# Three edits to an eight-core transformer-layer kernel: the rope's PSUM copy issued from ScalarE, one more wait ahead of the local attention, and the accumulate of the last feed-forward product written in place

## What is computed

```python
x = x + layernorm(attention(layernorm(x)))
x = x + layernorm(ffn(layernorm(x)))
```

```python
hidden = sigmoid(x @ q(w1).T) * (x @ q(w2).T)      # 5632 features
out = hidden @ q(w3).T
```

## Time and profile before

| | |
|---|---|
| median of 2 timed runs | 5871.52 us (5860.42 to 5882.63) |
| the profiled execution, its own time | 5821.73 us |
| its span, slowest core (7) | 5820.1 us; the eight cores 5774.1 to 5820.1 us |
| around the span | 1.6 us |
| busy on core 7 | PE 2818.6 us, DVE 2440.4 us, ACT 858.0 us, POOL 271.8 us |

### The profile page before, as it was taken

The page is one execution under the profiler, slowest core; times in us unless marked ns, Lnnn a source line. Parts: engine busy times, 40 slices in busy tenths (PEclk is TensorE's granted clock), DMA queues, the critical chain, the costliest instruction groups (busy, mean ns, idle before and its releaser), DMA issues.

```text
span 5820.1 us, 37163 instructions; the slowest of 8 cores (5774.1 to 5820.1 us)
## 1 busy us (share of the span) xinstructions
PE 2818.6 (48%) x11251; PEld 1090.7 (19%) x11251; DVE 2440.4 (42%) x3412; ACT 858.0 (15%) x1049; POOL 271.8 (5%) x518
## 2 busy tenths in 40 slices
PE   1556555556555522222222223657467676745553
PEld 1111111111111111111111111103223232322221
DVE  5322222222222244444444443004554545467887
ACT  1211122221122211111111111431100000000001
POOL 0000000000000001111111110000000000000000
PEclk9776666667766655555555555558688888877777
DMA  5211111111111033333333332013122222222221
GB/s 117 44 23 23 29 23 20 20 20 24 30 25 19 7 86 76 76 76 76 76 76 76 76 77 49 0 32 92 58 94 94 92 97 91 98 94 80 73 73 72
DMA packets 107475, 346.76 MB, mean 60 GB/s; under 512 B 12432, under 2 KB 69904, under 8 KB 78480
## 3 DMA queue, kind: packets, MB, share of 16 engines
q0 software_dynamic: 74016, 107.77, 12.8%
q1 hardware_dynamic: 17712, 123.38, 5.9%
q10 hardware_dynamic: 15552, 113.25, 5.5%
HBM read 443.71 MB, written 8.39 MB: 78 GB/s over the span
## 4 chain that ended last, share of the span: by engine, by line
PE 43%; DVE 27%; DMA 12%; ACT 9%; issue 8%; DVEq 1%; POOL 0%; ACTq 0%; POOLq 0%; SPq 0%
DMA AB<-w_t 10%; ACT MID L467 8%; PE pSA L888 7%; PE pSB L888 5%; DVE STT L281 4%; DVE STT L299 4%; PE pSA L450 3%; PE pAVB L497 3%; PE pAVB L394 3%; PE pT L345 3%; PE pSA L394 3%; PE pSA L969 2%; PE pG L516 2%; PE pSA L665 2%; PE pSB L394 2%
## 5 line engine op out<-in xcount | busy, mean ns | idle before, releaser
L345 PE MATMUL pT<-IDE,MID 128*128 128x128 bf16 x1216 | 153.8, 306 | 1233.2 <-DVE MID L325 1155.1
L281 DVE TENSOR_REDUCE STT<-AB 128x1 f32<-128x704 bf16 x384 | 340.1, 886 | 508.7 <-DMA AB<-w_t 495.2
L888 PE MATMUL pSA<-MID,WQS 128*128 128x512 bf16 x1408 | 400.4, 455 | 283.7 <-DVE WQS L871 283.7
L467 ACT ACTIVATE MID<-pSA,BIA 128x1024 bf16<-128x1024 f32 x212 | 236.3, 1115 | 1533.0 <-PE pSB L450 1533.0
L497 PE MATMUL pAVA<-MID,AB 128*65 128x512 bf16 x424 | 209.8, 595 | 353.7 <-ACT MID L467 208.3
L345 PEld LDWEIGHTS pT<-IDE,MID 128*128 128x128 bf16 x1216 | 117.7, 138 | 1266.2 <-issue 1266.2
L475 DVE TENSOR_TENSOR MID<-MID,AUX 128x1024 bf16<-128x1024 bf16 x128 | 88.6, 692 | 620.7 <-ACT MID L467 620.6
L969 PE MATMUL pSA<-WQS,AB 128*128 128x512 bf16 x576 | 171.5, 429 | 307.8 <-DVE AUX L948 238.7
L888 PE MATMUL pSB<-MID,WQS 128*128 128x512 bf16 x1408 | 311.1, 379 | 0.0
L450 PE MATMUL pSA<-MID 64*128 64x512 bf16 x300 | 151.3, 605 | 304.6 <-DVE STT L288 287.1
L279 POOL DMA_DIRECT2D AB<-w_t x384 | 203.0, 529 | 1838.8 <-DVE STT L288 1787.0
(11 more groups left out here) (137 smaller groups left out, 4086.6 us busy)
## 6 DMA issues: line engine op xcount, KB each, us to landing
AB<-w_t POOLq DMA_DIRECT2D x384, 176.0 KB, 3.4
AUX<-w_t ACTq DMA_DIRECT2D x66, 1024.0 KB, 4.8
XS<-w_t SPq DMA_DIRECT2D x66, 1024.0 KB, 4.8
MID<-x_glob SPq DMA_DIRECT2D x36, 1024.0 KB, 6.3
XS<-x_glob ACTq DMA_DIRECT2D x36, 1024.0 KB, 4.8
WQS<-wq_t POOLq DMA_DIRECT2D x16, 512.0 KB, 6.0
WQS<-wk_t POOLq DMA_DIRECT2D x15, 512.0 KB, 5.0
WQS<-wv_t POOLq DMA_DIRECT2D x15, 512.0 KB, 5.0
```

The costliest lines, as they stand in the source:

```text
L281: em("V", lambda e, par=par: e.tensor_reduce(ACOL, absbuf(par), AX.X, ALU.add, apply_absolute_value=True))
L345: tok = em("T", lambda e, dc=dc, k=k: e.transpose(pT[:, k * 128:(k + 1) * 128], XLT[:, dc * 128:(dc + 1) * 128], IDE[:]), "T" if k == 7 el ...
L467: e.activation(expsl(hb, 0, par), pbuf[:], AF.Exp, bias=b, scale=0.125),
L888: e.matmul(pbank[:, th * 512:(th + 1) * 512], w12q(m, qpar)[:, dc * 128:(dc + 1) * 128], xln2(dc, th * 512, (th + 1) * 512), start=(dc == ...
```

## The change

1. In `rope_chunk` the copy out of PSUM is an ACT activation with the function Copy instead of a DVE copy. It waits on ACT for the product, for the last rotation matmul and for the DVE instruction that last read `RAW0` (a new entry `rope_V` in `state`); PE and DVE wait for ACT's token where they used DVE's own order. The shapes are 128x512 in the local stage and 128x256 in the global one. Everything else of the chunk stays on its engine.
2. Ahead of the loop over pairs PE waits for all that DVE and ACT have been given so far.
3. In the second feed-forward product the add of groups 1 to 8 writes straight into `acct`, which is also its second input; the copy behind it (L985) is gone, and the bank's token is the add's.

```diff
--- before.py
+++ after.py
@@ -329,6 +329,7 @@
             return tn
 
         state = {"evac": 0, "xg_war": 0, "xlt_war": 0, "rot_T": 0,
+                 "rope_V": 0,
                  "xs_v": [0, 0], "xs_a": [0, 0], "cg_war": [0, 0]}
 
         def ln_transpose_tile(src_ap, src_tok, dst3, dst_col, pp):
@@ -398,17 +399,21 @@
             return tok
 
         def rope_chunk(psum_ap, pkey, cos_ap, sin_ap, dst_ap, ptok, W=512):
-            wt("V", "T", ptok)
-            wt("V", "T", state["rot_T"])
-            t_raw = em("V", lambda e, ps=psum_ap, W=W: e.tensor_copy(
-                RAW0[:, 0:W], ps), "V")
-            wt("T", "V", t_raw)
+            wt("A", "T", ptok)
+            wt("A", "T", state["rot_T"])
+            wt("A", "V", state["rope_V"])
+            t_raw = em("A", lambda e, ps=psum_ap, W=W: e.activation(
+                RAW0[:, 0:W], ps, AF.Copy), "A")
+            wt("T", "A", t_raw)
             psum_wait(["pG"])
             t_rot = em("T", lambda e, W=W: e.matmul(
                 pG[:, 0:W], RP[:], RAW0[:, 0:W], start=True, stop=True), "T")
             state["rot_T"] = t_rot
-            em("V", lambda e, cos_ap=cos_ap, W=W: e.tensor_tensor(
-                RTMP[:, 0:W], RAW0[:, 0:W], cos_ap, ALU.mult))
+            wt("V", "A", t_raw)
+            state["rope_V"] = em("V", lambda e, cos_ap=cos_ap, W=W:
+                                 e.tensor_tensor(
+                                     RTMP[:, 0:W], RAW0[:, 0:W], cos_ap,
+                                     ALU.mult), "V")
             wt("V", "T", t_rot)
             em("V", lambda e, sin_ap=sin_ap, W=W: e.tensor_tensor(
                 RAW1[:, 0:W], pG[:, 0:W], sin_ap, ALU.mult))
@@ -546,6 +551,8 @@
             wload(i, order[i][1], order[i][0])
         next_w = 4
         wt("T", "V", tv_ones)
+        wt("T", "V", cnt["V"])
+        wt("T", "A", cnt["A"])
         t_attn_T = 0
         for p in range(NPAIR):
             sq, sk, sv = (3 * p) % 4, (3 * p + 1) % 4, (3 * p + 2) % 4
@@ -978,12 +985,11 @@
                                      acct(tc)[:, hs * 512:(hs + 1) * 512],
                                      pb), "V")
                     else:
-                        em("V", lambda e, tc=tc, hs=hs, pb=pb:
-                           e.tensor_tensor(
-                               TMP6, pb,
-                               acct(tc)[:, hs * 512:(hs + 1) * 512], ALU.add))
-                        tev = em("V", lambda e, tc=tc, hs=hs: e.tensor_copy(
-                            acct(tc)[:, hs * 512:(hs + 1) * 512], TMP6), "V")
+                        tev = em("V", lambda e, tc=tc, hs=hs, pb=pb:
+                                 e.tensor_tensor(
+                                     acct(tc)[:, hs * 512:(hs + 1) * 512], pb,
+                                     acct(tc)[:, hs * 512:(hs + 1) * 512],
+                                     ALU.add), "V")
                     PW[pk] = ("V", tev)
                 if glast:
                     pp = tc % 2
```

## The result

| | before | after |
|---|---|---|
| median | 5851.22 us (5804.93 to 5884.26, 10 runs) | 5845.42 us (5744.41 to 5897.85, 11 runs) |
| ratio, 95% interval | | **0.985 [0.98, 0.99]** |
| profiled execution, its own time | 5821.73 us | 5758.61 us |
| its span; mean of the eight cores | 5820.1; 5795.8 us | 5757.0; 5733.5 us |
| busy on the slowest core | PE 2818.6, DVE 2440.4, ACT 858.0 us | PE 2779.7, DVE 2299.2, ACT 915.5 us |

In some executions the cores of one die show a lower clock whatever the kernel is; the ratio leaves these out, so it is not the quotient of the two medians. The change is faster by 1.5%, within the 2% called "the same". The forecast was 0.992 of before. Times of before reach down to 5804.93 us and times of after to 5744.41 us, 60.5 us apart, and the two profiles are 63.1 us apart; the forecast had 45.3.

The account below looks back on a forecast made before the run. No engine is full on average; work passes hand to hand, with DVE pacing feed-forward groups 1 to 7. Terms 27.9 + 11.4 + 7.3 + 1.5 - 2.8 = 45.3 us less, median 5826 us, range 5785 to 5862 us.

Parts of the forecast that it names:

- The accumulate in place: Second feed-forward product: without the copy PE paces groups 1 to 7, saving 27.9 us; the last group saves 11.4 us.
- The mis-sized term: Groups 1 to 7 of the second feed-forward product become like group 0: 3.99 us less a group, 27.9 us.
- the other reading in the prediction: Same groups, read from first instruction to quantization, 39.76 against 35.42 us: 4.34 a group, 30.4 us as upper reading.
- The rope's copy on ACT, local: Local stage rope chunks, 128x512: ACT copy 597 ns instead of DVE's 692, all on the chain, 77 chunks, 7.3 us less.
- the rival with no gain on ACT: Rope chunks: handover or copy on ACT eats the 0.095 us; gain 36.5 us, median 5835 us; 10 in 100.
- The rope's copy on ACT, global: Global stage rope chunks, 128x256: ACT copy an estimated 378 ns instead of DVE's 425, 32 chunks, 1.5 us less.
- The wait ahead of the pairs: Start of local stage: PE's first product waits for DVE's last sum, starting at 165.2 instead of 162.4; costs 2.8 us once.
- The Square pass and the tables: Global Square pass some 10 us later, covered by ACT's idle time; table-switch rival, 122 us of loads, 2 in 100.
- The full price: Rival, second feed-forward product: DVE alone paces, 256 copies at 0.40 us give 102 us; median 5763 us; 2 in 100.
- The 13/16: Cited clock rule, second feed-forward groups: dense matmuls on three or more cores of a die; tile 1.33 us, median 5884 us.
- the only one that spoke of the clock: Rival, groups 1 to 7: PE loses clock without its rests; at 1.2 GHz median 6066 us, slower; 3 in 100.
- The base: Whole kernel: profiled 5821.7 us less 45.3 gives 5776.4, ratio 0.992, scaled onto the 5871.5 us median: 5826 us.

Follow-up runs that it names:

- e2_local: Kernel before with the rope copy on ACT for the 128x512 chunks only, plus the wait ahead of the pairs; ratio to before 1.0015 [0.9975, 1.0056].
- e6_order: Changed kernel with met waits moved ahead of late ones, and PE waiting only for the last transposed tile before the pairs; ratio to before 0.9868 [0.9807, 0.9929].

## Why the prediction was right and wrong

**The accumulate in place: right in mechanism, a little low in size.** PE took over at 1.08 us a tile with 0.39 us of idle time on DVE, as forecast. On the slowest core of each profile groups follow each other by (5604.52 - 5219.65) / 6 = 64.15 us instead of 68.19, 4.04 us a group against 3.99 forecast. Over all cores the mean went from 68.43 to 63.82 us, 4.61 a group, but before has in it two cores on which groups took 70.7 to 72.0 us at a granted clock of 0.81; without cores 4 and 5 it is 68.20, and the difference 4.38. For the seven groups that makes 30.7 us, and with the last group, 12 us against 11.4, 43 instead of 39.3. The mis-sized term was 27.9, which measured 30.7; the other reading in the prediction, 30.4, was right. The reason can be read off the prediction's rows: group 0 needed 28.78 us from its first quantization instruction to the next group's first add (5240.34 - 5211.56), the later groups 68.19 - 39.76 = 28.43, so the whole of group 0 was a slightly too long pattern for them. The add whose output is its own input lasts 692 ns, like the other.

**The rope's copy on ACT, local: wrong.** The step that failed is "all of it is on the chain, so 77 x 0.095 = 7.3 us go". The duration was right to the nanosecond (597), but the handover was taken as unchanged, though the rival with no gain on ACT had named it as a possibility. The order of instructions did show the new list of waits, and the prediction read it for the queue behind the instruction only, not for its price. A chunk became 0.05 us longer instead of 0.095 shorter, and idle time before the rotations rose by 4.0 us instead of falling by 7. The stage as a whole lost 8.8 us against the cores of before with an undisturbed clock, 7.7 in e2_local; e6_order takes it back.

**The rope's copy on ACT, global: right in what it counted, wrong in what it left out.** The copy fell by 42 ns a turn (383 against 378 forecast, and 425 before), which is the 1.5 us of the sum. The failed step is the sentence that the V products take one of two times "by the clock they find" and that "another draw moves the sum by 5 to 8 us". It is not left to a draw, and there are three cases, not two. The pause that the edit shortens comes directly ahead of the V product, and its length decides whether, in the turns where the clock is not up yet, it comes up within the V product (141 of 256 turns in after, none in before) or only behind it (5 and 140). In numbers: the 16 starts of a V product went from 2.49 to 1.887 us, 32 x 0.60 = 19.3 of the 25.1 us; the shorter pause itself is 2.2, and the remaining 3.6 are not assigned. The counts of that sentence were off as well: on core 7 it was 19 turns of 1.91 us and 13 of 3.62. The clue stood in the earlier trace rows: two V products of one shape with 1.91 and 3.62 us. The prediction never asked what PE did ahead of each.

**The wait ahead of the pairs: right.** The first product started at 164.99 us on core 1, and 2.8 us later as a mean, as forecast.

**The Square pass and the tables: right.** ACT is still idle in front of L315, and only single table loads stand in the trace, 109 copies or not:

```profile
2711.56 0.38 ACT L405 ACTIVATE MID<-pSA 128x256 bf16<-128x256 f32 x1 [9.44 <-PE pSA L672]
2712.03 1.91 ACT L306 ACTIVATE MID<-MID 128x2048 bf16<-128x2048 f32 x1
...
2738.76 0.29 ACT L315 ACTIVATE STT<-STT 128x1 f32<-128x1 f32 x1 [24.72 <-DVE STT L311]
```

The idle time was 34.84 us; the 10 us of delay were covered. The table loads among the groups by form, after:

```profile
L306 ACT ACT_TABLE_LOAD x1 | 1.3, 1283 | 18.1 <-DMA MID<-x_hal 18.1
...
L903 ACT ACT_TABLE_LOAD x1 | 1.3, 1283 | 18.9 <-PE pSA L895 18.9
...
L315 ACT ACT_TABLE_LOAD x1 | 1.3, 1283 | 1.3 <-DVE STT L311 1.3
```

Three single loads, and none at L405: the rule of the Trainium skill, page "ScalarE: Activation LUTs", section "Table sets: the hidden batching unit", agrees with this trace. By the other rule cited from that page the copies were estimated at 613 and 399 ns; the rows have 597 and 383, 16 less at both widths.

**The rivals.** The full price did not come: PE paces. The clock did not fall in the groups, with tiles 1.08 us apart to the end on every core of after. The 13/16 of the Trainium skill, page "TensorE: Matmul & The Clock Gate", section "Part 1: The HAM clock gate", is in the traces all the same: cores 4 and 5 of before were granted 0.81 in groups 4 and 5 among others, with tiles 1.31 us apart where 1.33 was estimated. The prediction looked at core 7 only. Where the page has the whole die held for as long as the load lasts, here it was two cores for a part of the stage, and none in after. The rival with no gain on ACT was nearest for the local stage; of the two causes it named, the copy and the handover, it was the handover. No rival had the clock rise; the only one that spoke of the clock looked for it in the groups, and only downwards.

**The base.** The sum was scaled onto the median of two runs, 0.85% above the profiled execution. Those two (5860 and 5883 us) lay 55 and 78 us above the least time of before, so the forecast time carried that as well. The spread of 10 runs, 79 us, is larger than any term of the sum.

## What to carry to other kernels

When a copy moves to another engine, count its new waits along with its duration: a met wait that stands behind the late one costs on the chain each time, and an early place for it (ahead of the last matmul, ahead of the late wait) took the price off the chunk, though of 17 us won in the chunks the local stage kept only 9. Where one product takes two different times in one trace, by the granted clock, look at what PE did just ahead of it and whether the change alters that pause, before calling it chance. And read the granted clock on all cores, not on the slowest alone, before a mean over the cores is used. A copy taken away from an engine that sets the pace by a margin of 0.11 us a tile gives back 0.11 us a tile, and the group that already runs without the copy shows the new pace.

## What the runs showed of the hardware

- A pause of PE ahead of a 16-matmul product of 256 columns changed its mean time from 1.89 to 2.63 us between pauses of 0.68 us (5 of 256 late) and 0.70 us (163 of 256). With the shorter pause the granted clock came up within the product in 141 turns, with the longer one in none. Why the step lies there was not tested.
- Stretches with a granted clock of 0.81 stood on two cores of a die in before (129 to 189 us a core) and on none in after; tiles of 5 matmuls of 512 columns were 1.31 us apart in them instead of 1.08.
- An already met wait behind the late one costs about 0.11 us in front of a PE matmul (0.251 against 0.144 us from the copy's end to the rotation) and part of 0.11 us in front of an ACT copy (0.595 against 0.484 us, where e6_order moved two waits; in the global turns 0.553 against 0.505).
- A PSUM copy to bfloat16 lasts 597 ns on ACT and 692 on DVE for 128x512, 383 and 425 ns for 128x256, 405, 423 and 464 ns on ACT for 280, 304 and 352 columns.
- DVE's add out of PSUM lasts 692 ns whether or not it writes onto its own second input.
